# Slot 0 written out by hand, unit 1's maxima in four banks, two output pieces instead of three on GpSimd

## The reference

```python
q, k, v = x @ Wq.T + bq, x @ Wk.T + bk, x @ Wv.T + bv      # 16 heads of 64
q, k = q*cos + rotate_half(q)*sin, k*cos + rotate_half(k)*sin
attn = softmax(q @ k.T / 8); out = (attn @ v) @ Wo.T + bo
x = layernorm(x + out)
gates = softmax(x @ gate_w); top 2 of 8 experts, tok_w = sum of their gates
y = sum over the chosen experts of gelu(x @ w1 + b1) @ w2 + b2
return layernorm(x + y * tok_w)
```

## Time and profile before

| | |
|---|---|
| median of 3 runs | 249.88 us (248.84 to 250.79) |
| the profiled execution | 248.74 us, its span 246.9 us |
| busy in the span | DVE 189.5 us (77%), PE 186.0 (75%), ACT 157.4 (64%), GpSimd 146.1 (59%) |
| GpSimd, longest idle stretches | 27.4 us before its first product, 19.8 us before the first output piece |

### The profile page before, as it was taken

How to read it: one execution, slowest core, us unless ns; L and a number is a source line. 1 busy time by engine, 2 the same in 40 slices (tenths; PEclk the granted TensorE clock), 3 DMA queues, 4 the chain that set the end, 5 groups by cost and what they waited for, 6 DMA issues and landing times.

```text
span 246.9 us, 5191 instructions
## 1 busy us (share of the span) xinstructions
PE 186.0 (75%) x1817; PEld 129.4 (52%) x1817; DVE 189.5 (77%) x539; ACT 157.4 (64%) x321; POOL 146.1 (59%) x114
## 2 busy tenths in 40 slices
PE   1467799839768987876887897687685779998960
PEld 0121246626555765655566576455564655665660
DVE  6685747667978889888998887989989558359653
ACT  2558575928967976986997696795375374372300
POOL 6000084979989798797978879780480501000992
PEclk9999999968997997999999799999999799999996
DMA  7031224312122121221312213122100000000112
GB/s 248 40 77 31 62 69 123 85 25 65 37 52 64 47 66 38 54 58 43 75 36 54 66 39 75 33 57 54 32 3 5 0 4 0 0 3 0 44 45 85
DMA packets 12638, 12.30 MB, mean 50 GB/s; under 512 B 3116, under 2 KB 11716, under 8 KB 12612
## 3 DMA queue, kind: packets, MB, share of 16 engines
q1 hardware_dynamic: 12468, 11.70, 18.2%
q10 hardware_dynamic: 144, 0.26, 0.3%
HBM read 2.40 MB, written 1.05 MB: 14 GB/s over the span
## 4 chain that ended last, share of the span: by engine, by line
DVE 31%; POOL 25%; PE 25%; ACT 6%; DMA 5%; issue 5%; POOLq 0%; DVEq 0%
POOL by_cos L860 9%; DVE row_max L1018 9%; POOL by_sin L860 9%; DVE roped L982 7%; DMA qk<-mT_sb 5%; PE ps_t L422 4%; POOL y_sb L946 4%; ACT raw L716 3%; PE ps_m L466 3%; PE ps_m L361 3%; PE ps_s L378 3%; PE ps_s L388 3%; DVE o_sb L1041 3%; PE ps_o L439 2%; DVE hs L1244 2%
## 5 line engine op out<-in xcount | busy, mean ns | idle before, releaser
L735 ACT ACTIVATE probs<-ps_t 128x512 bf16<-128x512 f32 x128 | 77.2, 618 | 43.6 <-PE ps_t L422 43.0
L1018 DVE TENSOR_REDUCE row_max<-ps_s 128x2 bf16<-128x512 f32 x124 | 83.4, 675 | 21.2 <-PE ps_s L388 12.7
L860 POOL TENSOR_TENSOR by_cos<-raw,in_b 128x1024 bf16<-128x1024 bf16 x26 | 55.2, 2122 | 40.6 <-DVE roped L982 38.4
L716 ACT ACTIVATE raw<-ps_m,bqk 128x256 bf16<-128x256 f32 x128 | 53.6, 487 | 12.5 <-PE ps_m L361 8.5
L422 PE MATMUL ps_t<-qk 128*128 128x256 bf16 x256 | 53.5, 294 | 8.4 <-DMA qk<-mT_sb 8.4
L388 PE MATMUL ps_s<-qk 128*128 128x256 bf16 x224 | 45.8, 289 | 16.8 <-DVE row_max L1018 16.0
L860 POOL TENSOR_TENSOR by_sin<-raw,in_b 128x1024 bf16<-128x1024 bf16 x26 | 55.2, 2124 | 0.0
L439 PE MATMUL ps_o<-v_sb,probs 128*128 128x65 bf16 x512 | 38.6, 200 | 0.4 <-ACT probs L735 0.4
L361 PE MATMUL ps_m<-in_b 128*128 128x256 bf16 x128 | 30.0, 331 | 10.9 <-DMA in_b<-in_packed_b 4.2
L439 PEld LDWEIGHTS ps_o<-v_sb,probs 128*128 128x128 bf16 x512 | 34.0, 103 | 7.3 <-issue 1.1
L422 PEld LDWEIGHTS ps_t<-qk 128*128 128x128 bf16 x256 | 24.4, 103 | 17.3 <-DMA qk<-mT_sb 10.4
(11 more groups left out here) (127 smaller groups left out, 241.0 us busy)
## 6 DMA issues: line engine op xcount, KB each, us to landing
qk<-roped SPq DMA_DIRECT2D x128, 64.0 KB, 2.0
in_b<-in_packed_b SPq DMA_DIRECT2D x1, 770.0 KB, 6.5
out<-y_sb SPq DMA_DIRECT2D x3, 256.0 KB, 2.1
in_f<-in_packed_f SPq DMA_DIRECT2D x1, 586.0 KB
in_b<-in_packed_b SPq DMA_DIRECT2D x1, 512.0 KB, 4.5
in_b<-in_packed_b ACTq DMA_DIRECT2D x1, 256.0 KB, 3.6
qk<-mT_sb SPq DMA_DIRECT2D x16, 4.0 KB, 1.7
out<-y_sb SPq DMA_DIRECT2D x2, 128.0 KB, 1.8
```

Of the source, the lines that this page charges most:

```text
L716: last = nc.scalar.activation(raw[:, u % 2, g, a, half, :], ps_m[bank][:, half * S:half * S + S], ACT.Identity, bias=bqk[:, a, chunk:chunk ...
L735: nc.scalar.activation(probs[:, h % 4].rearrange("p c s -> p (c s)"), ps_t[h % 2][:], ACT.Exp, scale=DH ** -0.5).then_inc(exp_done, 1)
L860: last = nc.gpsimd.tensor_tensor(by[:, g].rearrange("p a h s -> p (a h) s"), raw[:, u % 2, g].rearrange("p a h s -> p (a h) s"), table[:]. ...
L1018: nc.vector.tensor_reduce(row_max[:, u % 2, h % 4, h // 4, :], of_head[:].rearrange("p (t s) -> p t s", s=S), AX_X, ALU.max, negate=True). ...
```

## The change

- **Start of DVE's list.** The copy of the bias `bqk`, for which ACT's first reads wait, comes before the last two of DVE's four pad memsets, not behind them.
- **Unit 1.** GpSimd makes its two sine products; DVE keeps the cosine product and the rotation. Its eight maxima use four banks (`second_banks`: two of `ps_s`, and `ps_o`, where the products with v go), and DVE does them all after the rotation of unit 2. Unit 2's first three heads are done straight from `roped` too (`direct_maxima`).
- **Slot 0** is a list of its own on PE, ACT and DVE (`first_slot`). Unit 0's first two scores come ahead of unit 3's projections and of unit 1's maxima. `run` starts with slot 1. Unit 3's projections and values of unit 2 move into it.
- **Output bias.** It comes in slot 0 in `ps_m[1]`; `bv_rep` is loaded by a DMA of 256 KB ready-made rather than spread by ACT; `split_bias` comes after unit 4's products.
- **DMAs.** Four of unit 2's eight regroup DMAs are issued by ACT. The loads of `in_f` and `exp_of` move to the end of SP's slot 3.
- **End.** ON_POOL is 2, and DVE makes piece 2's last pass after the moments of piece 3.

```diff
-        ON_POOL = 3
+        ON_POOL = 2
@@ SP
+                if T == 3:
+                    sp.dma_start(in_f[:], packed_f).then_inc(in_late, 16)
+                    sp.dma_start(exp_of[:], expert_of).then_inc(in_late, 16)
             maxima_row(0)
+            sp.dma_start(bv_rep[:], repeated_bv).then_inc(bv_ready, 16)
             regroup(1)
-            regroup(2)
-            sp.dma_start(in_f[:], packed_f).then_inc(in_late, 16)
-            sp.dma_start(exp_of[:], expert_of).then_inc(in_late, 16)
+            sp.wait_ge(rope_ready, 6)
+            for g in range(2):
+                for half in range(2):
+                    sp.dma_start(qk[32 * half:32 * half + 32, 2, :, g],
+                                 roped[32 * g:32 * g + 32, 0, half]).then_inc(qk_in[2], 16)
+            slot(0, 0)
@@ PE
+            def direct_maxima(u, heads):
+                banks = second_banks if u == 1 else ps_s
+                pe.wait_ge(rope_ready, 2 * u + 2)
+                pe.wait_ge(max_done, UH if (u, heads[0]) == (1, 0) else UH * u + heads[-1] - len(banks) + 1)
...
+                if u == 0 and h in (0, 2):
+                    pe.wait_ge(max_done, 2 * UH - 1 + h // 2)
...
+            def first_slot():
+                scores(0, 0, 0)
+                scores(0, 1, 0)
+                project(3, 0, 0, 1)
+                project(3, 0, 1, 0)
+                direct_maxima(1, [0, 1, 2, 3])
+                scores(0, 2, 0)
+                project(3, 1, 0, 1)
+                project(3, 1, 1, 0)
+                scores(0, 3, 0)
+                value(2, 0, 1)
+                value(2, 1, 0)
+                direct_maxima(1, [4, 5])
+                biases()
+                scores(0, 4, 0)
+                direct_maxima(1, [6, 7])
+                project(4, 0, 0, 0)
+                project(4, 0, 1, 1)
+                times_v(0, 0, 0)
+                times_v(0, 1, 0)
+                scores(0, 5, 0)
+                turn_maxima(1, 0)
+                times_v(0, 2, 0)
+                times_v(0, 3, 0)
+                scores(0, 6, 0)
+                direct_maxima(2, [0, 1])
+                project(4, 1, 0, 0)
+                times_v(0, 4, 0)
+                scores(0, 7, 0)
+                project(4, 1, 1, 1)
+                times_v(0, 5, 0)
+                direct_maxima(2, [2])
@@ ACT
+            exp(0, 3, 0)
+            read_value(2, 0, 1)
+            read_value(2, 1, 0)
+            act.wait_ge(rope_ready, 6)
+            for g in range(2, 4):
+                for half in range(2):
+                    act.dma_start(qk[32 * half:32 * half + 32, 2, :, g],
+                                  roped[32 * g:32 * g + 32, 0, half]).then_inc(qk_in[2], 16)
+            read_bias()
+            read_proj(4, 0, 0, 0)
+            read_proj(4, 0, 1, 1)
+            exp(0, 4, 0)
@@ GpSimd
+            pool.wait_ge(rope_ready, 2)
+            for g in range(2):
+                pool.wait_ge(raw_ready, 6 + 2 * g)
+                nc.gpsimd.tensor_tensor(by_sin[:, g].rearrange("p a h s -> p (a h) s"),
+                                        raw[:, 1, g].rearrange("p a h s -> p (a h) s"),
+                                        sin_sb[:].unsqueeze(1).broadcast_to([P, 4, S]), ALU.mult).then_inc(first_sin, 1)
             for piece in range(4):
                 products(3, piece)
+            slot(0, 0)
+            split_bias()
@@ DVE
+            pads(0)
             dve.wait_ge(in_first, 16)
             nc.vector.tensor_copy(bqk[:], part_b("bqk").rearrange("p (a c) -> p a c", a=2)).then_inc(consts_ready, 1)
+            pads(1)
...
             moments(3)
+            normed(2)
             residual(4)
```

More of the change, by code:

```diff
@@ L271, in run @@
         def run(eng, slot):
-            for T in range(UNITS + 1):
+            for T in range(1, UNITS + 1):
                 slot(T, 0)
@@ L371, in maxima @@
             def maxima(u, h, it):
[L372 to L384 removed]
+                if h == 0 or (u, h) == (2, EARLY):
                     pe.wait_ge(qk_in[u % 4], copies_in(u))
@@ L404, in first_maxima @@
                                                   rows[:, 0, half, 1, h // 4, :],
+                                                  start=(half == 0), stop=(half == 1))
+                            if t == QT - 1 and half == 1:
+                                mm.then_inc(s_ready, 1)
+            def direct_maxima(u, heads):
+                banks = second_banks if u == 1 else ps_s
+                pe.wait_ge(rope_ready, 2 * u + 2)
+                pe.wait_ge(max_done, UH if (u, heads[0]) == (1, 0) else UH * u + heads[-1] - len(banks) + 1)
+                for t in range(QT):
+                    for half in range(2):
+                        for h in heads:
+                            rows = roped[32 * (h % 4):32 * (h % 4) + 32]
+                            mm = nc.tensor.matmul(banks[h % len(banks)][:, t * S:t * S + S],
+                                                  rows[:, u % 2, half, 0, h // 4, t * P:t * P + P],
+                                                  rows[:, u % 2, half, 1, h // 4, :],
                                                   start=(half == 0), stop=(half == 1))
@@ L960, in _, with pads @@
             nc.vector.memset(v_sb[:].rearrange("p b c h d -> p (b c h) d")[:, :, DH:DH + 1], 1.0)
-            for i in range(2):
+            def pads(i):
                 q_pad, k_pad = [qk[M_ROW:P, i, a].rearrange("p g j s -> p (g j s)").bitcast(U32) for a in range(2)]
@@ L1230, in _ @@
                 rope(1, k)
-            for h in range(EARLY):
-                row_maxima(1, h, 0)
             for k in range(4):
                 rope(2, k)
+            for h in range(UH):
+                row_maxima(1, h, 0)
+            read_mT(1, 0)
+            invert_sums(0, 0, 0)
+            normalise(0, 0, 0)
+            row_maxima(2, 0, 0)
+            row_maxima(2, 1, 0)
+            rope(3, 2)
+            rope(3, 3)
+            invert_sums(0, 1, 0)
+            normalise(0, 1, 0)
+            row_maxima(2, 2, 0)
+            invert_sums(0, 2, 0)
             run(dve, slot)
```

91 lines of the change are left out of this document (39 added, 52 removed).

## The result

The changed kernel takes 239.23 us (median of 4 runs, 238.31 to 241.27) where the kernel before took 250.33 beside it (248.84 to 251.45): ratio 0.957, 95% interval 0.949 to 0.965. In a later measurement it gave 239.46 against 249.28, ratio 0.963 (0.958 to 0.968). The profiled execution took 239.49, its span is 237.7; against the profiled 248.74 of before that is 9.25 us, where my parts sum to 7.6.

A forecast was written before the change was run, and what follows sets the result against it. It took a loop of GpSimd products and DVE rotations as the bound, no engine holding a third of the chain. 5.7 (slots) + 1.9 (end) = 7.6 us off 249.88 gave 242.3 us, 8-in-10 range 239.9 to 246.0.

The forecast's parts named there:

- Start, unit 0, units 1 and 2: Opening: DVE's first product 1.5 us earlier, at 6.8; unit 0's maxima end at 16.9; units 1, 2 rotated at 20.0, 23.8.
- The rival of VectorE and GpSimd in each other's way: Sine products and DVE hold each other up at units 1 and 2 and the end: 247.2 us; chance 0.07.
- Slot 0, "6.4 us earlier": Slot 0, ACT's path with four DMA issues at 2.6 us: unit 4's first GpSimd product at 36.9 instead of 43.27.
- signs of being wrong: Unit 4's products start after 39, distance from there to the end grows, or ACT's issues hold its exponentials over 3 us.
- The bias: GpSimd's 2.76 us of bias instructions after unit 4's products: 0.7 of the 6.4 lost, unit 6's rotation at 66.8.
- in_f load in slot 3: Load moved behind SP's slot 3, taken as 0; rival: delays unit 5's maxima by 2.5, 244.8, chance 0.04; 252.5, chance 0.02.
- Slots 3 to 16 keep their order and shift: 5.7: Later slots, code unchanged, keep their order and all move 5.7 us earlier.
- End: Output pieces: piece 4's residual no longer waits for GpSimd's last pass of piece 2; 1.9 us gained, lower bound 1.2.
- Base: Starting time of the sum: profiled execution 248.74 gives 241.1; it lies 1.1 below the median 249.88, which gives 242.3.

The follow-up runs named there:

- g3: Changed kernel with the old end (three last-step passes on GpSimd, piece 2's normalisation behind piece 4's residual): 241.80 us, ratio 0.968 to the kernel before.
- f1: The changed kernel measured again without any edit: 239.46 us (238.41 to 241.65).
- f3: Changed kernel with unread matrix products in TensorE's idle spells ahead of the sixth scores of slots 1, 3, 5, 7, 9, 11: 236.13 us, ratio 0.950 to the kernel before.
- g1: Kernel before with unread matrix products in TensorE's idle spells of the start, 5 to 30 us: 245.06 us, ratio 0.986.
- e4: Kernel before with the change's new end alone (ON_POOL 2, piece 2's last pass on DVE): 246.28 us, ratio 0.989.
- f2: Kernel before with unread matrix products in TensorE's idle spells ahead of the sixth scores of slots 1, 3, 5, 7, 9, 11: 246.70 us, ratio 0.991.
- h1: Kernel before with unread matrix products in the idle spells of both the start and slots 1 to 11: 243.53 us, ratio 0.977.
- h2: Changed kernel with unread matrix products in the idle spells of both the start (ten) and slots 1 to 11: 235.87 us, ratio 0.947 to the kernel before.

## Why the prediction missed

Two terms failed: slot 0, which is where most of the missing gain is in the repeats, and the loop taken as a piece of fixed length. The base came on top.

- **Start, unit 0, units 1 and 2: right.** Milestones within 0.4, and each part undone costs what it was priced at: 1.58 for the bias copy (1.5), 1.1 for the sine product (1.2). The rival of VectorE and GpSimd in each other's way did not come: the two sine products ran from 11.19 to 15.38 at their usual 2.1.
- **Slot 0, "6.4 us earlier": this step failed, its size is one draw.** The issues on ScalarE took 4.5 in the profile (0.73 + 3.73) rather than 2.6, and between 2.1 and 3.7 for the last three in others. PE's list ran in part at 0.22 a pair where I took 0.42 from the earlier trace rows. Unit 4's product came at 35.71 rather than 36.9, and in the repeat at 33.84: a lead of 7.56 and of 9.43. At unit 7, where I had 5.7, the lead is 5.9 to 6.1 in the profiles with the long issues (the first, g3) and 8.2 to 8.6 in those with the short ones (f1, f3). The row I priced with was true of its own moment only: the spacing is a state of TensorE. Fast spacing in the kernel before alone brings its unit 4 forward by 2.96 (g1), so part of the lead is slow spacing that the change escapes. One of my signs of being wrong did come: the four issues held ScalarE's list for more than 3 us, with its exponentials at 24.04 and next at 30.86.
- **The bias: right in outcome.** Between units 4 and 5 the lead fell from 7.56 to 6.27, and unit 6's rotation came at 66.65 (66.8). No sign of the in_f load in slot 3.
- **"Slots 3 to 16 keep their order and shift: 5.7": this step failed.** The lead was 5.86 at unit 7, as forecast, and grew to 7.35 at unit 15 and 7.14 at the first output piece. Unmoved code has no fixed length: without added products eight slots take 81.7 to 83.3 in either kernel, from one execution to the next, and the pair that I compared drew 83.23 and 81.74. These 1.5 us are luck, not the change's: e4 has 81.76 with the code of before, f1 has 83.34 with the changed code, and with added products the distance of the two kernels does hold (f2 and f3, h1 and h2). The low-clock stretches behind the 1.5 stood in the windows of before, where I had not read PEclk.
- **End: right, slightly low.** 2.1 from both sides (e4, g3) against 1.9.
- **Base.** The sum missed the profiled execution by 1.65: 1.3 between unit 7 and the first output piece, 0.16 ahead of unit 7, 0.2 at the end. I then added 1.1, since before's profile lay that far below its median; the changed kernel's lies 0.3 above its own. That is the other 1.4 of the 3.1. The repeats of one kernel differ by 3 us; in the changed kernel's first runs 241.27 had a mean granted clock of 0.930, 238.31 and 238.96 had 0.958. A range needs that spread. In the later measurement the two medians lie 9.8 apart; 5.9 to 8.6 at unit 7 and 2.1 at the end make 8.0 to 10.7.

No rival had the clock. The profile of before spoke for one: PEclk under 0.6 behind idle spells, on a path that is a quarter PE. The Trainium skill (TensorE: Matmul & The Clock Gate, section "Part 1: The HAM clock gate") says that idle spells bring the slow state back. The traces agree for some spells: the clock fell behind 1.76 us in before and stayed at 1.00 behind 1.76 us in after and in e4. The same section puts the ramp's cost for modelling under 1% of a span. Here filling the start's idle spells brought unit 4 forward by 2.96 us, 1.2%, and the time by 1.4% (g1), so the measurement decides against it.

What stays open: why the kernel before stays at the slow spacing until 44 although its TensorE is busy without a gap from 32 to 44; why the clock falls behind a spell of 1.76 us in one execution and not in the next; what makes ScalarE's issues take 2.1 or 3.7; whether the instruction queue's packet makes the row late or both have one cause; and how the gain of slot 0 divides between the change's work and the clock.

## What to carry to other kernels

Before shifting a stretch rigidly, read its granted clock and the spacing of its matrix products; where it is slow behind an idle spell and PE is on the chain, its length can change from one execution to the next, and a forecast needs a case for it. Before putting a difference down to the change, profile each kernel twice: the same code differed by 1.5 us in eight slots here. To compare two kernels at one clock, put products into a free bank inside the idle spell, not behind it: that alone was worth 0.9 to 1.4% here, where such products placed behind the spell cost 1.7%. They also lengthen the program, which can move other things. A price read from one execution, of DMA issues above all, is one draw.

## What the runs showed of the hardware

- TensorE's granted clock fell to half behind idle spells of 1.76 to 4.72 us, and stretches such as 53.7 to 57.8 and 74.8 to 78.4 in the kernel before ran at it. It is not bound to follow: behind the same spells of 1.76 us it stayed at 1.00 in the changed kernel and in e4.
- In 4 to 44 us of the kernel before, the granted clock reads 1.00 while a pair of products of 256 columns and what follows it start 0.42 apart, 1.2 GHz. There only the spacing tells the state. From 31 to 40 in the changed kernel the clock reads 0.50 at the same spacing.
- The same three DMA issues on ScalarE took 2.14, 2.15, 3.44 and 3.73 us in executions with the same code ahead of them.
- A row of maxima, 4 KB, landed 1.7 us behind its issue in the median, and 2.27 to 2.95 where a packet of the instruction queue started 0.2 to 0.55 us behind the issue.
